# Sums over groups moved from DMA to VectorE, x loaded three items ahead, y accumulated by DMA onto a negative mean: a gated FFN stage with layernorm and projection

## What is computed

```python
xr = x.reshape(Bx, Tx, 8, LATENT)                         # LATENT 128
h = jnp.einsum('btel,elf->btef', xr, W1) + b1             # FFN 512
h = jax.nn.gelu(h, approximate=False)
y = jnp.einsum('btef,efl->btel', h, W2) + b2
y = y.reshape(Bx, Tx, Dx)
eo = jax.nn.silu(emb) @ emb_W + emb_b
scale, shift = jnp.split(eo[:, None, :], 2, axis=-1)
hn = _layernorm(y, ln_g, ln_b) * (1.0 + scale) + shift    # mean and variance over all 1024 features
proj = jax.nn.silu(hn) @ out_W + out_b
return x + proj
```

## Time and profile before

| | us |
|---|---|
| median of 3 runs | 740.33 |
| the profiled execution's own time | 743.72 |
| its span, first to last instruction | 741.7 |
| TensorE (PE) busy | 693.2 (93%) |
| VectorE (DVE) busy | 602.8 (81%) |
| ScalarE (ACT) busy | 488.9 (66%) |
| GpSimd (POOL) busy | 172.7 (23%) |

### The profile page before, as it was taken

How to read it: one execution, slowest core, us unless ns; L and a number is a source line. 1 busy time by engine, 2 the same in 40 slices (tenths; PEclk the granted TensorE clock), 3 DMA queues, 4 the chain that set the end, 5 groups by cost and what they waited for, 6 DMA issues and landing times.

```text
span 741.7 us, 8277 instructions
## 1 busy us (share of the span) xinstructions
PE 693.2 (93%) x2960; PEld 541.6 (73%) x2960; DVE 602.8 (81%) x663; ACT 488.9 (66%) x566; POOL 172.7 (23%) x116
## 2 busy tenths in 40 slices
PE   9999989999899997999998299999999999999998
PEld 6887577767677776767776188777777778777887
DVE  6866469687868767979886299999999999999952
ACT  6886567778777857786889066555566665666510
POOL 0010032040404103321112112333333322223200
PEclk9999999999999998999999599999999999999999
DMA  5799647978687598657679987777787777776651
GB/s 173 268 360 300 178 98 173 209 209 204 188 200 209 102 330 194 147 117 154 153 166 284 304 234 202 202 207 213 228 228 212 217 216 218 203 218 179 184 156 57
DMA packets 76120, 150.07 MB, mean 202 GB/s; under 512 B 12704, under 2 KB 50080, under 8 KB 72240
## 3 DMA queue, kind: packets, MB, share of 16 engines
q1 hardware_dynamic: 47760, 115.90, 46.6%
q0 software_dynamic: 19968, 33.56, 26.5%
q10 hardware_dynamic: 8352, 0.10, 0.6%
HBM read 76.11 MB, written 56.66 MB: 179 GB/s over the span
## 4 chain that ended last, share of the span: by engine, by line
DVE 34%; PE 27%; DMA 16%; issue 13%; ACT 9%; SPq 1%; DVEq 0%; POOL 0%; ACTq 0%; POOLq 0%
PE psum L1028 11%; PE psum L1006 8%; PE psum L988 7%; DMA xT_raw<-in_xT 5%; DVE res L852 5%; DMA y_sum<-y_stage 4%; ACT g_raw L514 4%; DVE yb L760 4%; DMA o_raw<-in_out_W 3%; DVE yb L782 3%; DVE d_lo L813 3%; DVE g_lo L728 3%; DVE a_lo L806 3%; DMA res<-out_b_all 2%; ACT g_hi L520 2%
## 5 line engine op out<-in xcount | busy, mean ns | idle before, releaser
L728 DVE TENSOR_TENSOR g_lo<-g_raw,g_hi 128x1024 fp32r<-128x1024 f32 x128 | 159.2, 1250 | 83.1 <-ACT g_hi L520 80.5
L514 ACT ACTIVATE g_raw<-psum,cols 128x1024 f32<-128x1024 f32 x128 | 142.6, 1114 | 42.9 <-DVE g_lo L728 24.3
L988 PE MATMUL psum<-xT_hi,W 128*128 128x512 f32 x508 | 139.8, 397 | 10.5 <-ACT g_raw L514 10.4
L1006 PE MATMUL psum<-g_hi,W 128*128 128x512 f32 x512 | 139.9, 395 | 5.8 <-DVE g_hi L726 3.3
L1028 PE MATMUL psum<-wa,d_hi 128*128 128x512 f32 x512 | 128.6, 394 | 17.8 <-DVE res L852 17.8
L1028 PEld LDWEIGHTS psum<-wa,d_hi 128*128 128x128 f32 x512 | 97.5, 191 | 38.7 <-issue 18.2
L988 PEld LDWEIGHTS psum<-xT_hi,W 128*128 128x128 f32 x508 | 95.3, 190 | 37.3 <-ACT g_raw L514 16.1
L1006 PEld LDWEIGHTS psum<-g_hi,W 128*128 128x128 f32 x512 | 96.5, 190 | 29.2 <-DVE g_hi L726 5.5
L852 DVE TENSOR_TENSOR res<-psum,res 128x512 f32<-128x512 f32 (+1 forms) x113 | 76.3, 675 | 37.3 <-PE psum L1028 20.9
L557 ACT ACTIVATE yb<-yb,mod_c,mod_a 128x256 f32<-128x256 f32 x120 | 62.4, 591 | 50.3 <-DVE yb L782 50.3
L444 POOL PARTITION_ALL_REDUCE var_all<-var_total x16 | 43.6, 2723 | 211.6 <-DVE var_total L773 211.6
(11 more groups left out here) (95 smaller groups left out, 921.8 us busy)
## 6 DMA issues: line engine op xcount, KB each, us to landing
y_scratch<-y_stage SPq DMA_DIRECT2D x32, 512.0 KB, 3.1
y_sum<-y_stage POOLq DMA_DIRECT2D x32, 512.0 KB, 8.4
yb<-y_scratch SPq DMA_DIRECT2D x16, 1024.0 KB, 6.4
res<-in_x SPq DMA_DIRECT2D x32, 512.0 KB, 4.1
res<-out_b_all POOLq DMA_DIRECT2D x32, 512.0 KB, 5.9
xT_raw<-in_xT SPq DMA_DIRECT2D x31, 512.0 KB, 5.5
out<-res SPq DMA_DIRECT2D x31, 512.0 KB, 5.5
emb_raw<-in_emb_W SPq DMA_DIRECT2D x8, 1024.0 KB, 9.7
```

The lines of the kernel that those rows point to most:

```text
L514: nc.scalar.activation(g_raw[:, m % 2], ring(m), ACT.Gelu, bias=cols[:, R_B1 + k:R_B1 + k + 1]).then_inc(gelu_done, 1)
L728: nc.vector.tensor_tensor(g_lo[:, m % 2], g_raw[:, m % 2], g_hi[:, m % 2].bitcast(F32), ALU.subtract).then_inc(glo_done, 1)
L988: mm = nc.tensor.matmul(ring(m)[:, half], W[:, g % WS, w, cut], v[:, n % 2, half], start=(k == 0), stop=(k == 2))
L1006: mm = nc.tensor.matmul(y_psum(n)[:, half], W[:, g % WS, w, cut], v[:, m % 2, half], start=(c == 0 and k == 0), stop=(c == C - 1 and k == 2))
```

## The change

What it does, in parts:

1. **Sums on VectorE.** For items 0 to 3 (group 0) stage_y writes straight into y_acc[t], one SBUF buffer of 4 KB per partition for each batch. For items 4 to 19 VectorE adds y_stage to y_acc (`add_y`, in chunk 2 of the item after). SP stores y_acc to y_sum (`store_sum`; batches 1 to 3 in iterations 14 to 16, batch 0 in iteration 21). Items 20 to 31 (groups 4 to 7 of batches 1 to 3) are still added by POOL's accumulating DMA, now with rows of 4 KB (y_sum is laid out [NT, P, TA]). mean_of for pairs 0 to 2 reads y_acc[0] in SBUF.
2. **x three items ahead.** SP's iteration n issues load_x(n+3), behind the same kind of wait (rest_x of two items before it).
3. **Other schedule of stage 1.** emb_W is loaded from iteration 0 on, VISIT is 5, W_ITEM and O_ITEM shift, the steps of an O item are spread over two items (chunks 0, 3, 4, 7), wc_out is stored three items after the O item.
4. **y onto a negative mean.** For pairs 2 to 15 ScalarE writes -mean/D into yb (`prefill`, two halves of 128x1024), and POOL loads y with an accumulating DMA (1 MB from DRAM to SBUF). centre stays for pairs 0 and 1 alone. In loop p: ScalarE has prefill(p+3) after round_a22(p+1); POOL has var_of(p+2), load_y(p+3), mean_of(p+4), add_bias twice; square(p+3) waits for y_landed.
5. **The change of stages.** The SBUF map is redrawn, so that t3's high part is loaded in iteration 31, res of pair 0 at iteration 29 and of pair 1 at 30, and POOL issues the first two add_bias before the sum of item 31. t3's low part, b22 and t4 are loaded after the end of stage 1 as before; t4's high part waits for the last y store and the last sum.

```diff
-    W_ITEM = {1: 1, 2: 3, 3: 5, 4: 7, 5: 10, 6: 13, 7: 17}
+    W_ITEM = {1: 1, 2: 3, 3: 5, 4: 9, 5: 12, 6: 13, 7: 17}
-    O_ITEM = {0: 8, 1: 11, 2: 14, 3: 18}
+    O_ITEM = {0: 6, 1: 10, 2: 14, 3: 18}
-    O_STEP = {(0, 0): (0, 1), (0, 2): (2, 3), (1, 0): (4, 5), (1, 2): (6,)}
-    VISIT = 6
+    O_STEP = {0: (0, 1), 3: (2, 3), 4: (4, 5), 7: (6,)}
+    VISIT = 5
+    ADD_ITEMS = list(range(NT, HG * NT + G - HG))
+    ADD_NO = {n: k + 1 for k, n in enumerate(ADD_ITEMS)}
+    DRAM_ITEMS = list(range(HG * NT + G - HG, N))
...
+        y_acc = [at(f"y_acc{t}", [P, TA], R0 + o * KB) for t, o in enumerate((126, 0, 4, 130))]
...
# SP
+            def store_sum(t, n):
+                sp.wait_ge(y_added, ADD_NO[n])
+                sp.dma_start(y_sum[t], y_acc[t][:]).then_inc(sum_stored[t], 16)
...
             for n in range(N):
-                if n + 2 < N:
-                    sp.wait_ge(xlo_done, n + 1)
-                    load_x(n + 2)
+                if n + 3 < N:
+                    sp.wait_ge(xlo_done, n + 2)
+                    load_x(n + 3)
...
                 if n == Y0_ITEM + 1:
...
                     load_y(0)
-                    load_y(2)
-                    sp.wait_ge(y_summed[0], 16 * sums_before(Y0_ITEM))
-                    load_sum(0)
...
-                if n == N - 2:
-                    sp.wait_ge(xlo_done, N)
-                    for q in range(2):
+                if n in (N - 3, N - 2):
+                    sp.wait_ge(s2_done, C * n)
+                    for q in (0, 1) if n == N - 3 else (2, 3):
                         load_res(q)
                 if n == N - 1:
-                    sp.wait_ge(s1_done, M)
-                    load_wc(C_T3, LO, t3)
-                    for q in range(2, 4):
-                        load_res(q)
+                    sp.wait_ge(s2_done, C * n)
+                    load_wc(C_T3, HI, t3)
...
             sp.wait_ge(glo_done, M)
-            load_wc(C_T3, HI, t3)
+            load_wc(C_T3, LO, t3)
...
-            load_y(3)
             for s in range(2):
                 sp.wait_ge(y_stored[s], 16 * (N // 2))
-            for t in range(NT):
-                sp.wait_ge(y_summed[t], 16 * G)
+            sp.wait_ge(y_summed[NT - 1], 16 * (G - HG))
             load_wc(C_T4, HI, t4)
+            load_sum(4)
             for p in range(NP):
-                if 1 <= p and p + 3 < NP:
-                    load_sum(p + 3)
-                    sp.wait_ge(s_sum, 4 * (p + 1))
-                    load_y(p + 3)
+                if 1 <= p and p + 4 < NP:
+                    load_sum(p + 4)
...
# POOL
+            def load_y(p):
+                pool.wait_ge(prefilled, 2 * (p - 1))
+                pool.dma_start(yb[p % 3][:], y_scratch[p], accum_op=ALU.add).then_inc(y_landed[p % 3], 16)
...
-                add_y(n)
-            pool.wait_ge(out_b_landed, 16)
-            for q in range(2):
-                add_bias(q)
+                if n == N - 1:
+                    pool.wait_ge(out_b_landed, 16)
+                    for q in range(2):
+                        add_bias(q)
+                if n in DRAM_ITEMS:
+                    add_y(n)
             for p in range(NP):
                 if p + 2 < NP:
                     var_of(p + 2)
-                if 1 <= p and p + 3 < NP:
-                    mean_of(p + 3)
+                if p + 3 < NP:
+                    load_y(p + 3)
+                if p + 4 < NP:
+                    mean_of(p + 4)
...
# ScalarE
+            def prefill(p):
+                act.wait_ge(mean_done, p + 1)
...
+                for h in range(2):
+                    nc.scalar.activation(yb[p % 3][:, half_of(h)], mean_all[:].unsqueeze(1).to_broadcast([P, HG, TP]),
+                                         ACT.Copy, scale=-1.0 / D).then_inc(prefilled, 1)
...
+                if (n, c) == (24, 2):
+                    prefill(2)
...
                     round_a22(p + 1)
+                if p + 3 < NP:
+                    prefill(p + 3)
...
# VectorE
+            def add_y(n):
+                t = ORDER[n][1]
+                dve.wait_ge(y_staged, n + 1)
+                if ORDER[n][0] == 1:
+                    dve.wait_ge(y_stored[t % 2], 16 * (t // 2 + 1))
+                nc.vector.tensor_tensor(y_acc[t][:], y_stage[:, n % 2], y_acc[t][:], ALU.add).then_inc(y_added, 1)
...
+                if c == 2 and n - 1 in ADD_NO:
+                    add_y(n - 1)
...
-                if (n, c) == (27, 1):
-                    centre(2, 0)
-                if (n, c) == (27, 3):
-                    centre(2, 1)
...
                 add(p, P6, z_ps(p), 0, right)
-                if p + 3 < NP:
-                    centre(p + 3, 0)
-                    centre(p + 3, 1)
                 add(p, P5, y5_ps, 1, right)
```

More of the change, by code:

```diff
@@ L185, in cond_ffn_program @@
         mean_done = sem("mean_done")
+        prefilled = sem("prefilled")
         centred = sem("centred")
@@ L238, in half_of, with staged_in, dram_sums @@
             return slice(h * HG, (h + 1) * HG)
-        def sums_before(n):
-            return sum(ORDER[k][1] == ORDER[n][1] for k in range(n + 1))
+        def staged_in(n):
+            g, t = ORDER[n]
+            return y_acc[t][:] if g == 0 else y_stage[:, n % 2]
+        def dram_sums(n):
+            return sum(ORDER[k][1] == ORDER[n][1] for k in DRAM_ITEMS if k <= n)
         P1, P2, P6, P5, P7, P3, P4 = range(1, 8)
@@ L422, in add_y @@
                 t = ORDER[n][1]
-                k = sums_before(n) - 1
                 pool.wait_ge(y_staged, n + 1)
-                place = y_sum[PT * t:PT * t + PT].rearrange("h p t -> p h t")
-                part = y_stage[:, n % 2].rearrange("p (h t) -> p h t", h=PT)
-                if k == 0:
-                    pool.dma_start(place, part).then_inc(y_summed[t], 16)
-                else:
-                    pool.wait_ge(y_summed[t], 16 * k)
-                    pool.dma_start(place, part, accum_op=ALU.add).then_inc(y_summed[t], 16)
+                if dram_sums(n) == 1:
+                    pool.wait_ge(sum_stored[t], 16)
+                else:
+                    pool.wait_ge(y_summed[t], 16 * (dram_sums(n) - 1))
+                pool.dma_start(y_sum[t], y_stage[:, n % 2], accum_op=ALU.add).then_inc(y_summed[t], 16)
             def mean_of(p):
-                pool.wait_ge(sum_landed, 16 * (p + 1))
-                if p >= 1:
-                    pool.wait_ge(centred, 2 * p)
-                nc.gpsimd.partition_all_reduce(mean_all[:], sum_in[:], P, bass.bass_isa.ReduceOp.add
-                                               ).then_inc(mean_done, 1)
+                if p < 3:
+                    pool.wait_ge(y_added, ADD_NO[Y0_ITEM])
+                else:
+                    pool.wait_ge(sum_landed, 16 * (p - 2))
+                if 1 <= p <= 2:
+                    pool.wait_ge(centred, 2 * p)
+                elif p > 2:
+                    pool.wait_ge(prefilled, 2 * (p - 2))
+                total = y_acc[0][:, p * TP:(p + 1) * TP] if p < 3 else sum_in[:]
+                nc.gpsimd.partition_all_reduce(mean_all[:], total, P, bass.bass_isa.ReduceOp.add).then_inc(mean_done, 1)
+            def load_y(p):
+                pool.wait_ge(prefilled, 2 * (p - 1))
+                pool.dma_start(yb[p % 3][:], y_scratch[p], accum_op=ALU.add).then_inc(y_landed[p % 3], 16)
             def var_of(p):
@@ L607, in _ @@
                     round_w(W_AT[n])
-                for i in range(2):
-                    if n - i in O_AT and (i, c) in O_STEP:
-                        for k in O_STEP[i, c]:
-                            round_o(O_AT[n - i], k)
+                for g, at_item in O_ITEM.items():
+                    for k in O_STEP.get(m - C * at_item, ()):
+                        round_o(g, k)
                 if (n, c) == (21, 3):
@@ L866, in _ @@
                     split_w(W_AT[n], c)
-                for i in range(2):
-                    if n - i in O_AT and (i, c - 1) in O_STEP:
-                        for k in O_STEP[i, c - 1]:
-                            split_o(O_AT[n - i], k)
+                for g, at_item in O_ITEM.items():
+                    for k in O_STEP.get(m - 1 - C * at_item, ()):
+                        split_o(g, k)
+                if c == 2 and n - 1 in ADD_NO:
+                    add_y(n - 1)
                 if (n, c) == (1, 2):
```

101 lines of the change are left out of this document (60 added, 41 removed).

## The result

The changed kernel takes 719.7 us, the median of 4 runs (718.5 to 720.47), against 740.47 before beside it: a ratio of 0.9717, 95% interval 0.97 to 0.9734, so 20.8 us faster. The forecast was 705.3 with a range of 691 to 720. The direction held, and the time lies just inside the range, 0.3 us from its edge. The size did not hold: 35 us were forecast. The profiled execution has a span of 718.8 us, 22.9 less than the 741.7 before.

| stretch | before, us | after, us | won | forecast |
|---|---|---|---|---|
| start to the eviction of item 31 | 401.05 | 386.15 | 14.9 | 17.0 |
| from there to the end of P4 of pair 0 | 38.0 | 34.7 | 3.3 | 15.6 |
| the rest | 302.6 | 298.0 | 4.6 | 2.4 |

The account below looks back on a forecast made before the run. Stage 1 was taken to lose 37 us, largely waiting for x, and VectorE to bound stage 2's pairs. Gains of 17.0 (stage 1), 15.6 (change of stages) and 2.4 (steady pairs), 35.0 in all, gave 705.3 us, range 691 to 720.

Parts of the forecast that it names:

- x three ahead: Stage 1: x gets 16.3 us of lead instead of 5.4, so ScalarE's 36.8 us wait should nearly all go.
- The adds: Stage 1, VectorE: 16 adds, 1.25 us each, lie beside TensorE's work except about 1 us over in four items.
- what stays lost in stage 1: Stage 1: 20 of 37 us stay lost (conditioning item 4, O steps 10, items 20 to 31 6); gain 17.
- Rival B: Stage 1: VectorE, with 20 us more, is late for g_lo; gain 6 instead of 17, 716 us; chance 0.15.
- The steady pair: Stage 2: period 20.1 us instead of 20.3 as the wait for y replaces VectorE's bound; 2.4 us won.
- The ring through load_y: Stage 2: rest_d, var_of, load_y, y's landing L, square, silu, round_d close a loop of period 12.1 + L, L 8.0 us.
- The fixed part: Stage 2 period without y's landing: 6.70 to var_of's end, squares 2.12, silu and round_d 3.02, semaphores 0.25; 12.1 us.
- Rival A: Stage 2: y lands in under 7 us, TensorE bounds at 19.04 to 19.1, 14 us more won, about 691; chance 0.12.
- Change of stages: Stage 1's end to P4 of pair 0: the 17.8 us bias wait goes, P4 ends near 22.4 us; 15.6 us won.
- 4.5 MB ... about 14 us from 2 us before the end, then t4's high part is issued: Change of stages: SP's queue of t3 low, b22, t4 low and last y store, at 2.98 us a MB.
- 2.5 MB at 5.9 us a MB, half of it ahead of t4: Change of stages, bound: engines shared with item 31's sum, pair 3's y and two bias adds leave a gain of 8.
- Rival D: Change of stages: t4 or pair 3's y comes so late that 8 us are won instead of 15.6; 713; chance 0.10.

Follow-up runs that it names:

- second experiment: The kernel before with one edit, x loaded three items ahead: ratio 0.9802 to the kernel before, 725.8 us.
- third experiment: The changed kernel with POOL's load_y(p+3) issued ahead of var_of(p+2) in each pair: ratio 0.9642 to the kernel before, 714.0 us.

## Why the prediction was right or wrong

**x three ahead: right.** The wait went whole, and stage 1 won 14.9 us of the 17 forecast. The second experiment shows that this part alone does it.

**The adds and "what stays lost in stage 1": right in size, partly by luck in its parts.** 20 of 37 us were forecast to stay, and 22 stay. The adds on VectorE and the new schedule together cost nothing net: with x three ahead stage 1 ends within 0.4 us of the same time with and without them (second experiment). Rival B, VectorE late for g_lo, did not come. The conditioning item kept 6.0 us against 4 forecast, and items 20 to 31 kept 5.6 against 6. The rest kept 10.7 against 10, and here lies the luck: item 14 alone took 17.6 us, 6.8 over, for a reason that the forecast lacked. Before, POOL waited for out_W's piece until 189.28 us and ran sum_o(2) behind the modulation, which began at 186.4. After, the piece had landed by 179.66 us, and sum_o ran on top of the modulation at 179.75. What a POOL that starts earlier would run beside was not asked.

**The steady pair: right.** The ring through load_y is what the trace and the third experiment show, and so is that the removal of centre is worth only a fraction of the 1.26 us a pair down to TensorE's bound. Landing 8.1 against 8.0 us; period 19.77 against 20.1. ScalarE's wait for y was put at some 3 us a pair and is 5.1. The fixed part was put at 12.1 and is 11.6, since squares, silu and round_d follow each other without a gap once all are ready. The gain in the last stretch, 4.6 us, is less than 12 x 0.53 = 6.4, since pair 1, which took 19.10 us before and not 20.3, now takes 19.67, and pair 2 takes 20.53. Rival A needed the last 0.7 us of the period; moving load_y in POOL's order gives them in most pairs. Its price is off by a slip: 12 x (20.1 - 19.04) is 12.7 us and not 14, so it stood for 692.6.

**Change of stages: this step failed.** The forecast put P4's end 22.4 us after the end of stage 1 and it came after 34.7. The term that was mis-sized is "4.5 MB ... about 14 us from 2 us before the end, then t4's high part is issued": 24.9 us were measured. The bytes on SP's queue were right, and their price was, if anything, too high. What was missing is the accumulating queue beside it, 3.02 MB and 15 us of engine time, all of it ahead of t4. The text knew it as a bound ("2.5 MB at 5.9 us a MB, half of it ahead of t4") and took the value without it; on a stretch where both queues are full it had to be in the sum, and the sum is then 11.8 + 15.0 = 27 us. The rows before the change held the same warning: there too t4's high part was issued 425.00 - 401.05 = 24 us after the end of stage 1, beside two bias adds and the last sum. By its own terms the forecast would have had 12 + 3.1 + 2 = 17 us and not 18 to 20, since the 14 us were counted from 2 us before the end. A second term was smaller: P4 itself was put at 2.9 us and took 4.9, as its first eight matmuls still take 3.75 us behind a wait of 6.9. The bias that was moved ahead of the end was not moved ahead of these transfers: it still ran after 386 us and cost 3.3 of them. Rival D, "the stall at the change only moves", is what happened, stronger than its own 8 us: of 17.8 us of waiting for the bias 3.3 came out as gain. Two experiments with different transfers taken out of the stretch, 1 MB of bias and 0.92 MB of y, show it by their sizes.

## What to carry to other kernels

Where a stretch is full on the DMA engines, add the engine time of every queue in it before you believe in a landing; here an accumulating DMA took twice the engine time of a plain one, 5.0 against 2.5 us a MB, on the same engines. Two parts of a change that shorten the same wait do not add: undo each alone, and do the simpler one alone on the old kernel: here the earlier load of x alone gave 14.7 of 21.0 us. When a transfer becomes faster, look at what its consumer now runs beside, on the ports that two engines share.

## What the runs showed that was not expected

A VectorE instruction of 128x64 takes 1317 ns beside a POOL tensor_tensor and 218 ns elsewhere, six times as long; the 128x1024 one of the earlier trace rows takes 2.31 us in place of 1.25, so the tiny instructions suffered more in proportion. The bias adds in steady pairs land in 8.0 to 12.0 us after their issue in place of 4.5 to 7.8 before, as they stand behind 1 MB of y on the same queue. That did not touch the pairs, since VectorE needs them later.
